# Bias of the feed-forward product: a ScalarE write into the bank of sums in place of a TensorE product

## What is computed

```
x = x + ga * attention(...)
h = layernorm(x) * (1 + cb) + sb
xd = quantise(h)            # blocks of 32 values onto a grid of 6-bit numbers, times the block's scale
wd = quantise(weight)       # 512 x 512, once
x = x + gb * (xd @ wd.T + bias)      # gb, bias: rows of 512; gb differs by batch
```

## Time and profile before

| | |
|---|---|
| median of 3 runs | 360.75 us (359.95 to 361.19) |
| the profiled execution | 359.63 us, its span 357.7 us |
| TensorE matmul busy | 318.3 us, 89% |
| VectorE busy | 283.9 us, 79% |
| ScalarE busy | 239.6 us, 67% |
| GpSimd busy | 234.0 us, 65% |
| mean granted TensorE clock | 0.967 of full |

### The profile page before, as it was taken

The page is one execution under the profiler, slowest core; times in us unless marked ns, Lnnn a source line. Parts: engine busy times, 40 slices in busy tenths (PEclk is TensorE's granted clock), DMA queues, the critical chain, the costliest instruction groups (busy, mean ns, idle before and its releaser), DMA issues.

```text
span 357.7 us, 6252 instructions
## 1 busy us (share of the span) xinstructions
PE 318.3 (89%) x2226; PEld 239.5 (67%) x2226; DVE 283.9 (79%) x499; ACT 239.6 (67%) x537; POOL 234.0 (65%) x139
## 2 busy tenths in 40 slices
PE   3788399878999989998999999978999989997894
PEld 1223266667898776786788678856887868675683
DVE  4994887965837997879898869797878889989932
ACT  3257566483978798689788889795779797241410
POOL 2063929059886896989599979994999399801000
PEclk9999589989999999999999999999899999998998
DMA  7997999973697097968598969497839791111122
GB/s 192 406 376 269 358 239 230 341 211 133 117 218 197 6 239 195 232 169 193 178 245 264 238 116 304 149 231 134 287 130 143 200 212 69 54 41 78 65 113 88
DMA packets 23797, 68.51 MB, mean 191 GB/s; under 512 B 2467, under 2 KB 2596, under 8 KB 19798
## 3 DMA queue, kind: packets, MB, share of 16 engines
q1 hardware_dynamic: 16224, 53.40, 44.3%
q0 software_dynamic: 7392, 14.68, 25.2%
q10 hardware_dynamic: 150, 0.02, 0.1%
HBM read 50.96 MB, written 17.14 MB: 190 GB/s over the span
## 4 chain that ended last, share of the span: by engine, by line
PE 42%; DVE 27%; ACT 12%; issue 7%; DMA 5%; POOL 4%; SPq 2%; DVEq 0%; ACTq 0%; POOLq 0%
PE ps L734 8%; PE ps L739 8%; PE ps L735 8%; DMA X<-in_wmod 5%; PE ps L717 4%; DVE Q L1200 4%; DVE amax L1181 4%; DVE DD L1207 3%; ACT U L490 3%; DVE XL L1157 3%; DVE X L1214 2%; ACT XH L458 2%; PE ps L645 2%; PE ps L820 2%; ACT unused L503 2%
## 5 line engine op out<-in xcount | busy, mean ns | idle before, releaser
L734 PE MATMUL ps<-WH,XH 128*128 128x512 f32 x256 | 108.4, 423 | 6.4 <-DVE X L1214 5.1
L735 PE MATMUL ps<-WL,XH 128*128 128x512 f32 x256 | 102.9, 402 | 0.0
L383 POOL TENSOR_TENSOR U<-U,c_bc 128x1024 f32<-128x1024 f32 x31 | 76.6, 2472 | 28.2 <-ACT U L490 28.1
L390 POOL TENSOR_TENSOR U<-U,sb_bc 128x1024 f32<-128x1024 f32 x31 | 74.2, 2394 | 4.8 <-POOL U L383 0.6
L1157 DVE TENSOR_TENSOR XL<-ps,XH 128x512 fp32r<-128x512 f32 x64 | 43.9, 686 | 38.2 <-ACT XH L458 38.1
L739 PE MATMUL ps<-WH,XL 128*128 128x512 f32 x256 | 70.6, 398 | 0.0
L458 ACT ACTIVATE XH<-ps 128x512 fp32r<-128x512 f32 x64 | 37.6, 587 | 48.6 <-PE ps L717 48.4
L490 ACT ACTIVATE U<-X,nmr,rstd 128x512 f32<-128x512 f32 x64 | 48.3, 808 | 30.7 <-DVE nmr L1174 28.1
L734 PEld LDWEIGHTS ps<-WH,XH 128*128 128x128 f32 x256 | 49.4, 193 | 17.9 <-DVE X L1214 6.8
L739 PEld LDWEIGHTS ps<-WH,XL 128*128 128x128 f32 x256 | 49.6, 194 | 11.2
L735 PEld LDWEIGHTS ps<-WL,XH 128*128 128x128 f32 x256 | 49.6, 194 | 8.8
(11 more groups left out here) (224 smaller groups left out, 426.5 us busy)
## 6 DMA issues: line engine op xcount, KB each, us to landing
X<-in_x SPq DMA_DIRECT2D x16, 1024.0 KB, 9.1
out<-X SPq DMA_DIRECT2D x15, 1024.0 KB, 5.5
X<-mod_scratch POOLq DMA_DIRECT2D x14, 1024.0 KB, 13.4
X<-in_wmod SPq DMA_DIRECT2D x2, 1024.0 KB, 14.7
sb_bc<-mod_scratch SPq DMA_DIRECT2D x7, 256.0 KB, 9.8
c_bc<-mod_scratch SPq DMA_DIRECT2D x7, 256.0 KB, 9.7
gb_bc<-mod_scratch SPq DMA_DIRECT2D x6, 256.0 KB, 7.8
X<-in_wmod SPq DMA_DIRECT2D x2, 512.0 KB, 4.4
```

Of the source, the lines that this page charges most:

```text
L383: nc.gpsimd.tensor_tensor(a, a, spread(c_bc[:, b % 2, :]), ALU.mult).then_inc(u_done, 2 if g == 0 else 1)
L390: nc.gpsimd.tensor_tensor(a, a, spread(sb_bc[:, b % 2, :]), ALU.add).then_inc(h_done, 2 if g == 0 else 1)
L734: M(bank, XH[:, n % 2, r], WH[:, b % 2, k, :], start=k == 0, stop=False)
L735: M(bank, XH[:, n % 2, r], WL[:, b % 2, k, :], start=False, stop=False)
```

## The change

For tiles 2 to 63 TensorE's line 742 is gone. In its place ScalarE copies the row `gb * bias`, which now lies on all partitions in `bias_bc` (two buffers, by batch), into the tile's bank before the product, and none of the twelve products starts a new sum: they all add onto what the bank holds. TensorE waits for this copy (`preset`) and no longer for the add itself; ScalarE waits for the add of tile n-2 and, once a batch, for the load of `bias_bc`. Tiles 0 and 1 keep a thirteenth product, now in plain fp32, with the row taken from `column_rows` (8 rows, picked by a column of `idf`), so `G`, `pick` and `gate_bias_rows` are gone. SyncE issues eight more row loads: those of batches 0 and 1 ahead of its loop, one each in later slots. Some semaphores are merged, which changes no order.

```diff
 # SyncE
             sp.dma_start(Wk[:], chunked(WkT)).then_inc(wk_in, 16)
             load_x(5)
+            sp.wait_ge(columns_out, 16)
+            for b in range(2):
+                mod_row(bias_bc[:, b, :], b, GBIAS, bias_in[b])
...
                     mod_row(gb_bc[:], b, GB, gb_in)
+                    sp.wait_ge(preset, 2 * TILES * (b - 1) - 2)
+                    mod_row(bias_bc[:, b % 2, :], b, GBIAS, bias_in[b % 2])
 # ScalarE
+            def preset_bias(n):
+                b = n // (2 * TILES)
+                act.wait_ge(bias_in[b % 2], 16 * (b // 2 + 1))
+                act.wait_ge(o_done, n - 1)
+                A.copy(ps[:, Y_BANK + n % 2, :], bias_bc[:, b % 2, :]).then_inc(preset, 1)
...
                 if q + 1 < LAST:
                     high_part(q + 1)
+                if 2 <= q + 1 < LAST:
+                    preset_bias(q + 1)
 # TensorE, product(n)
-                if n >= 2:
-                    pe.wait_ge(o_done, n - 1)
+                opens = n < 2
+                if not opens:
+                    pe.wait_ge(preset, n - 1)
                 pe.wait_ge(xh_done, n + 1)
                 for k in range(NC):
                     r = slice(k * P, (k + 1) * P)
-                    M(bank, XH[:, n % 2, r], WH[:, b % 2, k, :], start=k == 0, stop=False)
-                    M(bank, XH[:, n % 2, r], WL[:, b % 2, k, :], start=False, stop=False)
+                    M(bank, XH[:, n % 2, r], WH[:, b % 2, k, :], start=opens and k == 0, stop=False,
+                      skip_group_check=not opens)
+                    M(bank, XH[:, n % 2, r], WL[:, b % 2, k, :], start=False, stop=False, skip_group_check=not opens)
...
-                if n == 0:
-                    pe.wait_ge(g_rows, 4)
-                M(bank, pick[:, b:b + 1].to_broadcast([P, P]), G[:], start=False, stop=True).then_inc(y_done, 1)
+                if opens:
+                    pe.wait_ge(columns_cp, 1)
+                    m = M(bank, idf[0:B, 0:1].to_broadcast([B, P]), column_rows[0:B, :], start=False, stop=True)
+                m.then_inc(y_done, 1)
 # VectorE
-            def gate_bias_rows():
-                dve.wait_ge(cleared, 1)
-                dve.wait_ge(columns_cp, 1)
-                row = ps[0:B, COLUMN_ROWS, :]
-                W_.tensor_copy(G[0:B, :], row).then_inc(g_rows, 1)
-                dve.wait_ge(g_rows, 3)
-                TT(G[32:32 + B, :], row, G[0:B, :].bitcast(F32), ALU.subtract).then_inc(g_rows, 1)
...
-            gate_bias_rows()
```

More of the change, by code:

```diff
@@ L63, in build @@
         Wd = sb("Wd", [P, NC, D])
-        G = sb("G", [P, D], F32R)
-        pick = sb("pick", [P, B], F32R)
+        bias_bc = sb("bias_bc", [P, 2, D])
         onesr = sb("onesr", [P, P], F32R)
@@ L171, in build @@
         sb_in = [sem(f"sb_in{i}") for i in range(2)]
+        bias_in = [sem(f"bias_in{i}") for i in range(2)]
         wmod_in = [sem(f"wmod_in{i}") for i in range(7)]
@@ L181, in build @@
              "wv_in", "wo_in", "msp2_in", "head_stored", "cleared", "dve_step"))
-        (ga_mm, c_mm, s_mm, rows_mm, rows_cp, gate_mm, v_row, c_rows, s_rows, gb_col, rows_turned, columns_cp,
-         columns_out, cs_out, g_rows, u_first, h_first, xd1_done, s32_done) = (
+        (ga_mm, cs_mm, rows_mm, rows_cp, gate_mm, v_row, cs_rows, gb_col, rows_turned, columns_cp,
+         columns_out, cs_out, silu_rows, first_h, xd1_done, s32_done) = (
             sem(n) for n in (
[L186 to L190, removed]
+                "ga_mm", "cs_mm", "rows_mm", "rows_cp", "gate_mm", "v_row", "cs_rows", "gb_col",
+                "rows_turned", "columns_cp", "columns_out", "cs_out", "silu_rows", "first_h", "xd1_done", "s32_done"))
+        bd_done, hs_sa, bdm_done, gb_in, preset, plain_cp, w_copied = (
+            sem(n) for n in ("bd_done", "hs_sa", "bdm_done", "gb_in", "preset", "plain_cp", "w_copied"))
         (exp_c, silu_done, mod_mm, wd_done, wscaled, wt_mm,
@@ L593, in _ @@
             copy_rows(sb_rows, CS_ROWS, 4)
-            act.wait_ge(c_mm, 1)
-            A.copy(c_bc[:, 0, :], ps[:, C_BANK, :]).then_inc(c_rows, 1)
+            act.wait_ge(cs_mm, 1)
+            A.copy(c_bc[:, 0, :], ps[:, C_BANK, :]).then_inc(cs_rows, 1)
             normalise(0, 1)
-            act.wait_ge(s_mm, 1)
-            A.copy(sb_bc[:, 0, :], ps[:, S_BANK, :]).then_inc(s_rows, 1)
+            act.wait_ge(cs_mm, 2)
+            A.copy(sb_bc[:, 0, :], ps[:, S_BANK, :]).then_inc(cs_rows, 1)
             sums(1, 0)
@@ L699, in _ @@
             rows_of(3, CS_ROWS)
[L700 to L701 removed]
+            spread(c_rows_all, C_BANK, 3, cs_mm)
+            spread(sb_rows, S_BANK, 4, cs_mm)
             def transposes(n):
@@ L738, in product @@
                     r = slice(k * P, (k + 1) * P)
-                    M(bank, XL[:, n % 2, r], WH[:, b % 2, k, :], start=False, stop=False)
-                if n == 0:
-                    pe.wait_ge(g_rows, 4)
-                M(bank, pick[:, b:b + 1].to_broadcast([P, P]), G[:], start=False, stop=True).then_inc(y_done, 1)
+                    m = M(bank, XL[:, n % 2, r], WH[:, b % 2, k, :], start=False, stop=not opens and k == NC - 1,
+                          skip_group_check=not opens)
+                if opens:
+                    pe.wait_ge(columns_cp, 1)
+                    m = M(bank, idf[0:B, 0:1].to_broadcast([B, P]), column_rows[0:B, :], start=False, stop=True)
+                m.then_inc(y_done, 1)
             def project(bank, state, dg, row, signal):
@@ L908, in _ @@
             TT(cE[:], cE[:], cTs[:], ALU.mult).then_inc(silu_done, 1)
-            dve.wait_ge(small_in, 16)
-            TT(pick[:], idf[:, 0:B], idf[:, 32:32 + B], ALU.add).then_inc(g_rows, 1)
             def quantise(src, q8, nblk):
@@ L1009, in first_modulate @@
                 dve.wait_ge(z_done, HALF)
[L1010 to L1014, removed]
+                dve.wait_ge(cs_rows, 1)
+                TT(a, spread(C_BANK), a, ALU.mult).then_inc(first_h, 1)
+                dve.wait_ge(first_h, 1)
+                dve.wait_ge(cs_rows, 2)
+                TT(a, a, spread(S_BANK), ALU.add).then_inc(first_h, 1)
             def spread(bank):
```

23 lines of the change are left out of this document (11 added, 12 removed).

## The result

The kernel before took 360.97 us (median of 4 runs), the changed one 415.34 us (median of 4, 414.65 to 416.89). The ratio is 1.152 (95% interval 1.149 to 1.155): 54.4 us more, where 19.1 were forecast. The sign was right, the size was not, and 415.3 lies above the range's end of 391.

A forecast was written before the change was run, and what follows sets the result against it. The prediction saw no engine as the bound alone from 120 to 240 us, the chain changing hands every few tiles. Its terms, 17.0 + 1.3 - 0.7 + 5.0 - 2.3 - 1.2 = 19.1 us, gave 379.9 us, range 371 to 391.

The forecast's parts named there:

- Late row: At tile 2, ScalarE's first bank copy waits for the `bias_bc` load, landing at 73.6; all later work shifts 17.0 us.
- vanishes in the full queue: At the start, the row load's issue, later by 1.3 us, was taken not to delay its landing at 73.6.
- Taken from TensorE: 62 of 64 bias products go; 29 on the chain at 0.23 us each, 6.7 us at most.
- Added to ScalarE for every tile: From tile 2 on, one copy of 0.52 us a tile, which waits for the add of tile n-2.
- the middle: 120 to 240 us: +5.0 us net, bounds -2.5 (all copies hidden) to +14.6 (none hidden).
- such coupling in the rest of the stretch: 120 to 240 us, outside 149.6 to 171.7: copies waiting for VectorE's add, 2.5 us by judgement.
- two places before 90 us: A weight chunk's high part stands behind the waiting copy, VectorE's low part comes 0.65 later; two such places, +1.3 us.
- first rival: ScalarE bounds the middle, each slot lasting as long as the longer engine's part: +14.6 for +5.0, 389.5 us; chance 0.13.
- the argument from slack: Against ScalarE as bound from 120 to 240 us: heavy slots at different tiles, and ScalarE waited for 16.1 us there.
- From 240 us: From 240 us, ten bias products fewer on the chain, -2.3 us; ScalarE had room there (57.7 of 93).
- The clock behind the first wait: TensorE's idle stretch brings back the 1.2 GHz level, product 2 takes 5.2 us; VectorE hides it: 0, at most 2.5.

The follow-up runs named there:

- e1: The changed kernel with the first two row loads of `bias_bc` issued early, right behind the store of the rows that they read: 396.76 us, ratio 1.099.
- e2: The changed kernel with ScalarE's bias copy moved behind the weight chunk in its slot, the late row kept: 391.95 us, ratio 1.084.
- e3: The changed kernel with both edits, rows loaded early and bias copy behind the weight chunk: 374.48 us, ratio 1.037.
- e11: The changed kernel with the first two row loads moved ahead of the two 1 MB loads, still behind the wait for `mod_mm` 2: 405.48 us, ratio 1.128.
- e4: The kernel before without the bias product of tiles 2 to 63 and nothing in its place: 356.03 us, ratio 0.988.
- e6: The kernel before, bias product kept, plus ScalarE's wait for the add and 62 copies into a spare tile, ahead of the weight chunk: 395.49 us, ratio 1.096.
- e5: The kernel before, bias product kept, plus 62 ScalarE copies into a spare tile with no wait for VectorE: 368.03 us, ratio 1.022.
- e7: The kernel before, bias product kept, plus ScalarE's wait for the add and 62 copies into a spare tile, behind the weight chunk: 372.35 us, ratio 1.033.
- e9: The kernel before, bias product kept, plus only ScalarE's wait for the add of tile n-2, ahead of the weight chunk, no copy: 379.64 us, ratio 1.054.

## Why the prediction was right, and where it was wrong

**Late row: right.** It forecast 17.0 us, and 18.6 (after less e1) and 17.5 (e2 less e3) were measured. The signs came: a wait of 22.4 us for the DMA (some 18 were forecast, which was too low by the prediction's own rows: from 53.5, where the sums started, to 73.6 is 20.1), a landing 14.7 us after the issue (11 to 14), TensorE idle for 15.9 (some 13), matmuls 0.43 apart, the low part at 79.50 (77). The 2 us on top are the landing at 75.7 instead of 73.6; "vanishes in the full queue" was wrong: the 1.3 us by which the fp32 products were to delay the issue did show, as 1.2 (the 1 MB load of `x` is issued at 60.50 instead of 59.33). In e11 the same load took 6.1 us ahead of the 1 MB loads, against 14.7 behind them. The rule of the ring order in the Trainium skill that the prediction weighed ("DMA: Bandwidth & Descriptors", section "Queues, rings and completion order") is borne out by this.

**Taken from TensorE: right by itself, not shown in the changed kernel.** It was -0.7, -2.0, -2.3 and -1.2, so 6.2; e4 gives 4.7 (2.0 to 6.6), in a kernel without the new waits. With the new waits the runs show no gain (e1 less e6, +1.3).

**Added to ScalarE for every tile: wrong, and this is the step that failed.** It held two things. The copies as load were priced at 0.52 a tile with most of them hidden; e5 found 7.9 us for all of them, nearly all in the middle as forecast and within the bounds given for it (-2.5 to +14.6). The wait was priced by the phrase "for such coupling in the rest of the stretch I add 2.5 (by judgement, not from a row)", with 1.4 for one tile, and with nothing from 240 us on. The rows for a better price were at hand: the prediction had written, for two places before 90 us, that the high part of a weight chunk stands behind the copy which waits for the add, and that VectorE comes 0.65 later. The same order holds in all 32 slots with a chunk, and in 28 of them ScalarE has two operations for it and not one. In each of these VectorE is 0.6 us past its add when it wants the chunk, and ScalarE needs three operations of 0.52 from there: 1.0 to 1.2 us, 28 times, is about 31 us, and 32.3 were measured as wait (3.5 before) and 22 to 23 as time (e1 less e3, e6 less e7). Against the forecast's 3.9 for this tie in the middle (1.4 and 2.5) and nothing behind it stand e9's 19.5 us for the wait alone and e6's 35.4 for wait and copies. The error was to name a mechanism at two places and not count the others.

**Range and first rival.** The rival with ScalarE as the bound of the middle had the right image, "the copy ties ScalarE to VectorE's add at the slot's start, and the low part ties VectorE to ScalarE", and its sign came (the stretch from tile 13 to 40 was over 10 us longer, 22.4). But its price, 14.6 us, counted only work, as if a tie could cost no more than the copies' own time; e9 shows a tie of no work at 19.5. It was also confined to the middle, while 13 of the 28 slots lie behind it. Its other sign failed: ScalarE was to be busy for 115 or more of 120 us from tile 13 on, and was for 101. The middle became longer by waiting, not by a full engine. For the same reason the argument from slack misled me ("the two have their heavy slots at different tiles, and ScalarE waited for 16.1 us there"): those idle stretches were ScalarE's lead over VectorE, which let VectorE find its inputs ready. The wait took away the lead: ScalarE's idle time ahead of its high parts fell from 48.4 us to 14.4, and 62.7 us of waiting for VectorE's add came in its place.

**From 240 us: wrong in sign.** -2.3 was forecast, +13.1 came; ScalarE's room there (57.7 of 93) was taken for cover. It did cover the copies (e5: 97.3 us from high part 40 to add 59, against 97.6 before) and not the wait (e9: 102.4). Room does not help against a wait for the other engine.

**The clock behind the first wait: 0, right as far as it went.** Product 2 took 5.0 us (5.2 forecast) and ended at 81.3, while VectorE came to its add only at 86.23. What I had not asked is whether later gaps bring the lower level back. Ten products took over 4.2 us after against three before, each some 1.6 us more than the usual 3.0. In e1 and e3 there are eight each, although they differ by 22 us, so there the clock doesn't explain the price of the order. In the other two pairs the count falls with it, from ten to four (changed kernel and e2) and from eight to five (e6 and e7), so a part of the price may run through the clock there. How large that is stays open; no run separates it.

## What to carry to other kernels

Before a wait is put into an in-order engine's queue, list what is queued behind it and who needs that, in every slot of the loop and not only where the profile's chain happens to pass; multiply the gap by the number of slots. An engine's idle time is no free room if it is the lead by which its neighbour finds inputs ready. Here a wait with no work cost 19.5 us ahead of two operations and some 6 behind them, and the operation that was removed had been worth about 5.

## What the runs showed of the hardware

- A load of 256 KB took 14.7 us from issue to landing behind two loads of 1 MB in the same queue, and 6.1 when issued ahead of them at nearly the same moment (61.05 and 59.61).
- 62 copies of 128x512 with 37.8 us of busy time on ScalarE cost 7.9 us where they waited for nobody (e5).
- The mean granted clock of TensorE was 0.924 in the changed kernel, where TensorE was busy for 79% of the span, and 0.967 before, at 89%. Between them it rises with the busy share only roughly: 0.940 at 82% (e1), 0.951 at 81% (e2), 0.954 at 85% (e3).
